# Cross attention's step in another order: output product three tiles behind, second weighted values in the next step, normed rows in two buffers

## The reference

```
h = layernorm(x)
q = heads(h @ Wq + bq) / 4 ; k = heads(ctx @ Wk + bk) ; v = heads(ctx @ Wv + bv)   # 16 heads of 16
s = einsum('bhqd,bhkd->bhqk', q, k), -1e20 where a key is masked
a = softmax(s) ; o = einsum('bhqk,bhkd->bhqd', a, v)
x = x + tanh(g) * (o @ Wo + bo)
```

## Time and profile before

| | us |
|---|---|
| median of 3 runs | 780.43 (779.02 to 782.97) |
| the profiled execution | 787.23 |
| its span, first to last instruction | 785.5 |
| the loop over steps, first L787 to last L863 | from 126.0 to 302.2 |
| TensorE busy in the span | 675.3 (86%) |

### The profile page before, as it was taken

One profiled execution on the slowest core, in us unless ns is written; L12 is line 12 of the kernel. 1 busy time (PEld: TensorE's weight loads), 2 busy tenths in 40 slices (PEclk: granted clock), 3 DMA queues, 4 the chain that ended last, 5 costly groups with the idle time before them and its releaser, 6 DMA issues.

```text
span 785.5 us, 14749 instructions
## 1 busy us (share of the span) xinstructions
PE 675.3 (86%) x5303; PEld 463.8 (59%) x5303; DVE 425.5 (54%) x1290; ACT 328.0 (42%) x703; POOL 260.7 (33%) x377
## 2 busy tenths in 40 slices
PE   5999998999999984864999999997599999993773
PEld 3565654555555553642666666656478888872663
DVE  5645546677778755784222222112368887673544
ACT  2343434777776771523222222220645555411640
POOL 4101102334443432005345545233101343244465
PEclk9999998899999997976999999999699999996997
DMA  8669943566665215952254694325313472123661
GB/s 265 197 180 244 261 117 89 99 131 128 132 120 130 65 58 168 95 181 70 35 123 93 165 321 99 65 27 125 117 55 108 144 249 98 58 75 109 193 200 65
DMA packets 105040, 103.12 MB, mean 131 GB/s; under 512 B 22102, under 2 KB 95321, under 8 KB 104964
## 3 DMA queue, kind: packets, MB, share of 16 engines
q1 hardware_dynamic: 95752, 85.72, 42.1%
q0 software_dynamic: 9216, 16.46, 9.4%
HBM read 60.15 MB, written 42.25 MB: 130 GB/s over the span
## 4 chain that ended last, share of the span: by engine, by line
PE 38%; DVE 6%; issue 5%; ACT 4%; DMA 4%; POOL 2%; SPq 0%; another core or an unknown queue 0%; POOLq 0%; DVEq 0%; ACTq 0%
PE pc L1486 9%; PE pc L1463 9%; PE pc L950 3%; PE pc L2013 2%; PE pc L2006 2%; DMA g_rows<-scratch_slots 1%; PE pc L1482 1%; PE pc L2004 1%; PE pc L2073 1%; ACT enc L1865 1%; PE pc L1466 1%; PE pc L2286 1%; PE pc L1450 1%; PE pc L1973 1%; DVE d_w_c L1782 1%
## 5 line engine op out<-in xcount | busy, mean ns | idle before, releaser
L617 ACT ACTIVATE probs<-pb,b_key_cols 128x512 f32<-128x512 f32 x128 | 92.8, 779 | 17.0 <-PE pb L787 17.0
L484 DVE TENSOR_REDUCE neg_max<-pb 128x4 f32<-128x512 f32 x128 | 81.7, 680 | 3.0 <-PE pb L767 3.0
L1366 POOL DMA_INDIRECT scratch_resid<-y,k_idx x32 | 54.7, 1708 | 86.1 <-DVE y L1416 85.8
L1434 ACT ACTIVATE mid<-pc,b_up 128x512 f32<-128x512 f32 x40 | 27.4, 687 | 112.8 <-PE pc L1463 109.9
L1486 PE MATMUL pc<-w_dn,mid 128*128 128x256 f32 x320 | 73.3, 384 | 0.0
L1463 PE MATMUL pc<-gT,w_up 128*128 128x512 f32 x160 | 71.5, 603 | 0.9 <-DVE gT L1398 0.9
L1486 PEld LDWEIGHTS pc<-w_dn,mid 128*128 128x128 f32 x320 | 59.5, 190 | 12.7 <-issue 5.3
L1463 PEld LDWEIGHTS pc<-gT,w_up 128*128 128x128 f32 x160 | 31.0, 194 | 36.9 <-issue 36.5
L1416 DVE TENSOR_SCALAR y<-pc,gate 128x256 f32<-128x256 f32 x32 | 15.5, 484 | 65.1 <-PE pc L1486 47.2
L1357 POOL DMA_INDIRECT rows<-scratch_rows,k_idx x32 | 31.2, 975 | 57.8 <-DVE k_idx L1240 48.4
L365 POOL CAST nm_parts<-neg_max 128x16 bf16<-128x16 f32 x32 | 6.3, 198 | 125.4 <-DVE neg_max L484 125.4
(11 more groups left out here) (342 smaller groups left out, 1424.1 us busy)
## 6 DMA issues: line engine op xcount, KB each, us to landing
qs<-scratch_qparts SPq DMA_DIRECT2D x48, 128.0 KB, 4.5
ks<-scratch_kparts SPq DMA_DIRECT2D x48, 128.0 KB
w_dn<-in_W_down SPq DMA_DIRECT2D x8, 640.0 KB
scratch_slots<-s_zero SPq DMA_DIRECT2D x1, 4160.0 KB, 20.6
c_in<-in_ctx SPq DMA_DIRECT2D x8, 512.0 KB, 6.7
s_x<-in_x SPq DMA_DIRECT2D x8, 512.0 KB, 7.1
scratch_ctxT<-cT SPq DMA_DIRECT2D x8, 512.0 KB, 6.4
scratch_resid<-s_x SPq DMA_DIRECT2D x16, 256.0 KB, 3.1
```

The costliest lines, as they stand in the source:

```text
L484: V.tensor_reduce(neg_max[:, h:h + 4], ps_s[b][:].rearrange("p (h k) -> p h k", h=4), AX.X, ALU.max, negate=True).then_inc(max_s, 1)
L617: A.activation(probs[2 * u + b][:], ps_st[b][:].rearrange("p (h q) -> p h q", h=4), ACT.Exp, bias=key_cols[:, 1, t:t + 1], scale=key_cols[ ...
L1366: pool.indirect_dma_start(out=T["resid"], out_offset=bass.IndirectOffsetOnAxis(ap=S["idx"][:, e, c:c + 1], axis=0), in_=y[e % 2][:, c, :], ...
```

## The change

TensorE, step s: `context(s-1, 1)`, the second weighted values, follows `shifted(s, 0)`, where it was ahead of the step's end for tile s; then come the output product of tile s-3 (it was s-2), `scores(s+3, 0)`, `shifted(s, 1)`, `max_T(s+2)`, `context(s, 0)`, turning of `ctxT` of s-1, `scores(s+3, 1)`, and turning of `attn` of s-2 (it was s-1). ScalarE: `attnT` of s-3, `exponentials(s, 0)`, `ctxT` of s-1, `max_out(s+2)`, `exponentials(s, 1)`. VectorE: residual of s-3, `row_max(s+3, 0)`, statistics of s-3, `normalise(s-1)`, moments of s-3, `row_max(s+3, 1)`. SyncE stores `x1` one step later. `attn` has two buffers. No instruction is added or removed.

```diff
--- before.py
+++ after.py
@@ -140,7 +140,7 @@
         nmT = two("nmT", [2 * HEADS, P], BF16)
         probs = [sb(f"probs{i}", [P, 4, P]) for i in range(4)]
         ctxT, inv_sum = sb("ctxT", [P, 4 * P]), sb("inv_sum", [P, HEADS])
-        attn, attnT = sb("attn", [P, D]), sb("attnT", [P, HALVES, P])
+        attn, attnT = two("attn", [P, D]), sb("attnT", [P, HALVES, P])
         vareps1 = two("b_vareps", [P, QUAD])
         stats1 = two("b_stats", [P, 6])
 
@@ -307,7 +307,7 @@
                         load_queries(q, s % QUAD // 2)
                     if s % QUAD in (1, 3):
                         load_keys(q, s % QUAD // 2)
-                t = s - 2
+                t = s - 3
                 if is_tile(t) and t % 2:
                     sp.wait_ge(x1_s, t + 1)
                     sp.dma_start(x1_t[:, t - 1:t + 1, :], x1[:, t - 1:t + 1, 0:D]).then_inc(x1_out, 16)
@@ -491,9 +491,9 @@
                     dve.wait_ge(attn_s, t)
                 V.reciprocal(inv_sum[:], heads[:, :, HD]).then_inc(inv_s, 1)
                 dve.wait_ge(inv_s, t + 1)
-                if t >= 1:
-                    dve.wait_ge(aT_ps, t)
-                V.tensor_tensor(attn[:].rearrange("p (h d) -> p h d", h=HEADS), heads[:, :, 0:HD],
+                if t >= 2:
+                    dve.wait_ge(aT_ps, t - 1)
+                V.tensor_tensor(attn[t % 2][:].rearrange("p (h d) -> p h d", h=HEADS), heads[:, :, 0:HD],
                                 inv_sum[:].unsqueeze(2).broadcast_to([P, HEADS, HD]), ALU.mult).then_inc(attn_s, 1)
 
             def residual(t):
@@ -559,15 +559,16 @@
             values(q, 1)
             dve.wait_ge(tanh_s, 1)
             for s in range(0, END):
-                if is_tile(s - 2):
-                    residual(s - 2)
-                    statistics1(s - 2)
+                if is_tile(s - 3):
+                    residual(s - 3)
                 if is_tile(s + AHEAD):
                     row_max(s + AHEAD, 0)
-                if is_tile(s - 2):
-                    moments1(s - 2)
+                if is_tile(s - 3):
+                    statistics1(s - 3)
                 if is_tile(s - 1):
                     normalise(s - 1)
+                if is_tile(s - 3):
+                    moments1(s - 3)
                 if is_tile(s + AHEAD):
                     row_max(s + AHEAD, 1)
 
@@ -644,24 +645,24 @@
             max_out(1)
             act.wait_ge(key_s, 1)
             for s in range(0, END):
+                t = s - 3
+                if is_tile(t):
+                    act.wait_ge(aT_ps, t + 1)
+                    if t >= 1:
+                        act.wait_ge(o_ps, t)
+                    A.activation(attnT[:], ps_aT.rearrange("p (h t) -> p h t", h=HALVES), ACT.Copy).then_inc(aT_s, 1)
+                if is_tile(s):
+                    exponentials(s, 0)
                 t = s - 1
                 if is_tile(t):
                     act.wait_ge(av_ps, 2 * t + 2)
                     if t >= 1:
                         act.wait_ge(ctxT_ps, t)
                     A.activation(ctxT[:], ps_ctx[:], ACT.Copy).then_inc(ctxT_s, 1)
-                if is_tile(s):
-                    exponentials(s, 0)
                 if is_tile(s + 2):
                     max_out(s + 2)
                 if is_tile(s):
                     exponentials(s, 1)
-                t = s - 1
-                if is_tile(t):
-                    act.wait_ge(aT_ps, t + 1)
-                    if t >= 1:
-                        act.wait_ge(o_ps, t)
-                    A.activation(attnT[:], ps_aT.rearrange("p (h t) -> p h t", h=HALVES), ACT.Copy).then_inc(aT_s, 1)
 
         @block.tensor
         def _(pe):
@@ -770,8 +771,8 @@
 
             def max_T(t):
                 pe.wait_ge(nm_s, t + 1)
-                if t >= 4:
-                    pe.wait_ge(aT_s, t - 3)
+                if t >= 5:
+                    pe.wait_ge(aT_s, t - 4)
                 if t >= 1:
                     pe.wait_ge(nmT_s, t)
                 M.transpose(ps_nmT, nm_parts[:].rearrange("p a b h -> p (a b h)"), ident_b[:]).then_inc(nmT_ps, 1)
@@ -854,7 +855,9 @@
             for s in range(0, END):
                 if is_tile(s):
                     shifted(s, 0)
-                t = s - 2
+                if is_tile(s - 1):
+                    context(s - 1, 1)
+                t = s - 3
                 if is_tile(t):
                     pe.wait_ge(aT_s, t + 1)
                     if t >= 1:
@@ -862,12 +865,13 @@
                     for h in range(HALVES):
                         ins = M.matmul(ps_o, attnT[:, h, :], wo[:, h, :], start=(h == 0), stop=(h == HALVES - 1))
                     ins.then_inc(o_ps, 1)
-                if is_tile(s + 2):
-                    max_T(s + 2)
                 if is_tile(s + AHEAD):
                     scores(s + AHEAD, 0)
                 if is_tile(s):
                     shifted(s, 1)
+                if is_tile(s + 2):
+                    max_T(s + 2)
+                if is_tile(s):
                     if s == 0:
                         pe.wait_ge(v_s, 2 * QUADS)
                     context(s, 0)
@@ -881,14 +885,12 @@
                     ins.then_inc(ctxT_ps, 1)
                 if is_tile(s + AHEAD):
                     scores(s + AHEAD, 1)
-                if is_tile(s):
-                    context(s, 1)
-                t = s - 1
+                t = s - 2
                 if is_tile(t):
                     pe.wait_ge(attn_s, t + 1)
-                    pe.wait_ge(nmT_s, min(t + 4, TILES))
+                    pe.wait_ge(nmT_s, min(t + 5, TILES))
                     for h in range(HALVES):
-                        ins = M.transpose(ps_aT[:, h * P:(h + 1) * P], attn[:, h * P:(h + 1) * P], ident[:])
+                        ins = M.transpose(ps_aT[:, h * P:(h + 1) * P], attn[t % 2][:, h * P:(h + 1) * P], ident[:])
                     ins.then_inc(aT_ps, 1)
 
 
```

## The result

The changed kernel takes 755.75 us (median of 4 runs, 755.38 to 757.5) against 781.4 (4 runs, 779.02 to 782.97). The ratio is 0.968, 95% interval 0.965 to 0.971: 3.2% faster, 25.7 us. The profiled execution took 757.5 and its span is 755.7. Behind L562 the lines have moved by one to three, and ScalarE's two copies have changed places: the output product is L866, `shifted` L788, scores L768, turned maxima L778, weighted values L801, turning of `ctxT` L884 and of `attn` L893, exponentials L618, `attnT` L653, `ctxT` L661.

A forecast was written before the change was run, and what follows sets the result against it. The prediction took one chain through TensorE and ScalarE to bound the old step, and TensorE's work the new one at 4.70. Gains of 14.0 (25 steps), 3.6 (end) and 2.0 (start) sum to 19.6: 761.0 us, range 753 to 771.

The forecast's parts named there:

- one chain of 5.25: Old steady step: weighted values, turning, `attnT`, `ctxT`, exponentials, second `shifted` and second exponentials follow without a gap, 5.25 us.
- TensorE's sum: New steady step: TensorE's own work, added from start to start, gives 4.67 us; 4.70 taken as the step.
- the exponentials' chain: New step: turned maxima, their copy, second exponentials, then the next tile's first `shifted`; 4.56 us, 0.11 under TensorE's sum.
- cover of 0.05: VectorE's first maxima let the second scores start at 3.92 us into the step; TensorE comes to them at 3.97.
- five neighbours: New pairs of adjacent TensorE work that no profile row shows; at most 0.09 us cheaper, a step of 4.58.
- The last three steps: Steps 29 to 31, without scores: gains of 1.03, 1.33 and 1.33 us, put together at 3.6.
- The first tiles: Loop's start, partly at half clock: a gain of 2.0 us, between 0 and 4.
- The tail: From the last weighted values on, one serial chain in both orders: no gain, 1 us either way.
- The busy share: Rival, chance 0.14: TensorE's 94% leaves only its idle time, a step of 4.92 us, total 768.
- The maxima's transfers: Small SyncE transfers: 4.4 us, hidden within 6.23. Rival that they come late, chance 0.05: 790.
- The clock: Rival, chance 0.12: one more stretch at half clock in the fill costs some 3 us, total 764.
- Nothing happens: Rival, chance 0.05: another unseen wait of about 5.2 us stands right behind the first, total 779.

The follow-up runs named there:

- `values_back`: Changed kernel with the second weighted values back at the end of their own step: 778.32 us, 0.998 of the kernel before.
- `tile_nearer`: Changed kernel with output product two tiles behind and turning of the normed rows one, as before the change: 776.86 us, 0.995 of the kernel before.
- `copy_first`: Changed kernel with ScalarE's copy `ctxT` back ahead of the first exponentials: 787.1 us, 1.009 of the kernel before.
- `maxima_first`: Changed kernel with the maxima turned ahead of the first scores: 759.27 us, 0.973 of the kernel before.
- `moves_held`: Changed kernel with the maxima's two small transfers issued only after the second shifted scores of the tile before: 794.94 us, 1.017 of the kernel before.
- `one_buffer`: Changed kernel with one buffer for the normed rows, whose product waits for the turning of the tile before: 755.01 us, 0.968 of the kernel before.
- `turning_first`: Changed kernel with the turning of the normed rows ahead of the second scores: 755.3 us, 0.968 of the kernel before.

## Why the prediction was right

**The chain.** The prediction read the old period as one chain of 5.25 and not as TensorE's load. The change cut it and the period fell by 0.71. `values_back` and `tile_nearer` each put back one half: steps of 5.13 and 5.16, near the 5.12 and 5.17 worked out by the same way of adding links.

**What bounds the step in its place.** Here the working was off in size and in order. TensorE's sum was put at 4.67 and, with a margin, taken as the bound at 4.70; the exponentials' chain at 4.56, "hidden, barely"; VectorE with a cover of 0.05. The exponentials' chain measured 4.55, but its 4.56 was right by luck: TensorE's part was 0.09 too long (2.64 for 2.55), the part from there to the next `shifted` 0.08 too short (1.92 for 2.00). TensorE's sum was the mis-sized term: the turning of `ctxT` is held at 0.70; at the 0.59 that it takes where nothing holds it (204.28 to 204.87 in `copy_first`), the starts sum to 4.44. Two of the five neighbours that stood in no row were cheaper than their nearest rows: scores ahead of `shifted` 0.23, not 0.33, and the turned maxima between `shifted` and weighted values 0.01, not 0.17. The bound below, -0.09 for all five, was too narrow: it is -0.26 for these two. So TensorE isn't the limit, its second scores wait 0.11 for VectorE's maxima, and the two chains through the other engines set 4.55 together. The prediction had named this wait, and a period short of 4.6, as signs that it was wrong; both came. What was right is the chain that was cut; what bounds the new step was not. 25 steps x 0.15 = 3.8 of the 5.2 us between the forecast of 761.0 and the result come from this.

**The ends.** The last three steps measured 4.32, 4.02 and 3.94, the worked-out ones were 4.23, 3.93 and 3.93. The gain was still put too high, 3.6 for 2.5 (its three terms even add up to 3.7), by a slip: step 31 was counted with a full 5.26, but the earlier trace rows end at the last weighted values, 4.31 after its start. The first tiles gave 4.6, above the 0 to 4 that was allowed. TensorE's clock was at half there from 132 to about 142 us before the change, and from about 131 to 137 after it; how much of the 4.6 is the clock's and how much the chain's was not tested. The tail gave 0.7, within its 1. So the loop gave 6.0 more than the sum of 19.6: 3.7 in the steady steps, 2.6 in the first and 0.7 in the tail, less 1.1 in the last three.

**The rivals.** *The busy share*: a step of 4.92 was its claim; TensorE's share went from 94 to 99% and the step to 4.55, and in `maxima_first` the share is higher still at a longer step, 4.71. The page "Perfetto Trace Analysis" of the Trainium skill (Identifying the Most-Contended Engine) calls this share no good measure of the distance to the limit. The traces here agree: by this share 0.33 of each step's 5.26 was not busy, and the step fell by 0.71. *The maxima's transfers*: 2.54 from issue to reader by `moves_held`, against 4.4 in the sum and 8.06 as the bound, with 6.2 allowed: hidden by far. The fixed cost of about 2.0 that the page "DMA: Bandwidth & Descriptors" of the Trainium skill gives (Anatomy of one DMA) is for transfers issued by GpSimd, and it includes the set-up. The prediction's estimate of 3.3 added it behind both of SyncE's issues and is 0.8 above the 2.54; from the start of the second issue (216.98) to the reader it is 1.9, near the page's figure. *The clock*: full in the steady part, and back sooner in the fill. *Nothing happens*: no wait of 5.2 stood behind the first in the full change; each half alone had one. The prediction's claim that the second buffer of `attn` is needed was wrong: `one_buffer` is as fast.

## What to carry to other kernels

If the period of a pipelined loop stays the same where an engine runs out of work at its end, that engine doesn't set it; add up the links of the one circle that does, and do the same for every circle that the new order leaves. Cutting one is worth only as much as the next is shorter, and here two halves of a change, each worth 0.2 to 0.5%, made 3.2% together, while one copy of a third engine left in its old place turned it into a loss of 0.9%. Once several circles lie within some 0.1 us of each other, further moves mostly trade one wait for another; the wait that a view names is then not the only one, as a lone swap that removes it shows.

## What the runs showed of the hardware

- Eight small bfloat16 matmuls hold TensorE 0.23 when eight more such follow (scores to `shifted`, 206.94 to 207.17), 0.33 ahead of a float32 group and 0.32 ahead of the single turning of the maxima (207.17 to 207.49), though that is bfloat16 too. This single one costs 0.01 between bfloat16 matmuls and a float32 group (207.49 to 207.50), and 0.16 to 0.17 ahead of another bfloat16 group.
- Where TensorE waited for exponentials, the second `shifted` and the weighted values start 0.05 after their recorded end, the first `shifted` of a tile 0.13 to 0.14 after it (204.76 to 204.90 in `turning_first`). It goes by the reader and not by whether the exponentials had waited: in `copy_first` they start right behind a copy, and the second `shifted` still follows after 0.05 (203.31 to 203.36). Why the readers differ was not tested.
- Two transfers of 4 KB from one place of the on-chip memory to another are readable 2.54 after the first issue begins and 1.2 after the second issue ends (216.32 and 217.64 to 218.86 in `moves_held`).
